# Attention with a feed-forward part in float32: four of eight key tiles in high and low parts, and rotations spread one per chunk

## The reference

```python
qkv = einsum('bsd,od->bso', xn, w_qkv)            # 16 heads of 128, q, k and v
q, k = rope(q), rope(k)                           # x*cos + rotate_half(x)*sin
attn = softmax(einsum('bqhd,bkhd->bhqk', q, k) / sqrt(128))
out = einsum('bhqk,bkhd->bqhd', attn, v)
att = einsum('bso,do->bsd', out.reshape(B, S, 2048), w_out)
h = gelu(xn @ dequantised(up) + up_bias)          # 256 -> 1024, weights rounded to MXFP4
ffn = h @ dequantised(down) + down_bias           # 1024 -> 256
```

## Time and profile before

| | us |
|---|---|
| median of 3 runs | 2452.34 (2449.78 to 2453.95) |
| the profiled execution's own time | 2450.13 |
| its span, first to last instruction | 2448.3 |
| PE busy | 2417.7 (99%) |
| DVE, POOL, ACT busy | 1912.9, 1728.9, 1677.9 |
| mean granted TensorE clock | 0.998 |

### The profile page before, as it was taken

The page is one execution under the profiler, slowest core; times in us unless marked ns, Lnnn a source line. Parts: engine busy times, 40 slices in busy tenths (PEclk is TensorE's granted clock), DMA queues, the critical chain, the costliest instruction groups (busy, mean ns, idle before and its releaser), DMA issues. The chain is left out here.

```text
span 2448.3 us, 42812 instructions
## 1 busy us (share of the span) xinstructions
PE 2417.7 (99%) x13168; PEld 2124.8 (87%) x13168; DVE 1912.9 (78%) x2671; ACT 1677.9 (69%) x3039; POOL 1728.9 (71%) x1358
## 2 busy tenths in 40 slices
PE   6999999999999999999999999999999999999999
PEld 5888888888888888888888888888888888888888
DVE  6778788777877877787787778778777877877776
ACT  7767777776766777676677767667776766777533
POOL 4778877777777777777777777777777777777331
PEclk9999999999999999999999999999999999999999
DMA  4766666667666666667666666667676565666742
GB/s 140 185 170 161 171 158 178 162 162 195 182 161 149 158 152 157 157 148 195 179 161 153 157 157 148 161 149 183 165 186 157 148 162 149 157 153 161 230 153 69
DMA packets 400878, 396.72 MB, mean 162 GB/s; under 512 B 38656, under 2 KB 383104, under 8 KB 400768
## 3 DMA queue, kind: packets, MB, share of 16 engines
q1 hardware_dynamic: 400768, 395.67, 63.0%
HBM read 91.43 MB, written 35.65 MB: 52 GB/s over the span
## 5 line engine op out<-in xcount | busy, mean ns | idle before, releaser
L947 DVE TENSOR_REDUCE neg_max<-s_ps 128x1 f32<-128x1024 f32 x512 | 621.0, 1219 | 291.2 <-PE s_ps L1244 290.5
L1244 PE MATMUL s_ps<-seq_parts 128*128 128x512 f32 x3072 | 826.8, 408 | 1.4 <-DVE seq_parts L1111 0.8
L758 ACT ACTIVATE probs<-s_ps,neg_max 128x1024 f32<-128x1024 f32 x512 | 570.6, 1114 | 365.5 <-DVE neg_max L947 361.8
L1326 PE MATMUL o_ps<-keys_first,v_rows 128*128 128x256 f32 x3072 | 707.7, 380 | 1.3 <-ACT v_rows L725 1.3
L957 DVE STREAM_TRANSPOSE turned_blocks<-probs 128x1024 f32<-128x1024 f32 x512 | 630.6, 1237 | 60.6 <-ACT probs L758 38.1
L1244 PEld LDWEIGHTS s_ps<-seq_parts 128*128 128x128 f32 x3072 | 571.8, 188 | 117.2 <-ACT probs L758 1.5
L1326 PEld LDWEIGHTS o_ps<-keys_first,v_rows 128*128 128x128 f32 x3072 | 566.9, 190 | 68.6 <-ACT v_rows L725 1.7
L608 POOL TENSOR_TENSOR keys_first<-keys_first,seq_parts 128x512 fp32r<-128x512 f32 x256 | 332.4, 1298 | 320.2 <-ACT seq_parts L764 320.0
L587 POOL TENSOR_TENSOR rope_a<-rope_a,cos 128x512 f32<-128x512 f32 x252 | 325.3, 1291 | 176.9 <-ACT rope_b L740 176.7
L601 POOL TENSOR_TENSOR seq_parts<-rope_a,seq_parts 128x512 fp32r<-128x512 f32 x252 | 359.4, 1426 | 95.2 <-ACT seq_parts L750 95.1
L1244 PE MATMUL slot_ps<-seq_parts,w_parts 128*128 128x512 f32 x1506 | 387.9, 393 | 0.0
(11 more groups left out here) (118 smaller groups left out, 2597.2 us busy)
## 6 DMA issues: line engine op xcount, KB each, us to landing
keys_first<-turned_blocks SPq DMA_DIRECT2D x2048, 128.0 KB, 2.7
w_parts<-w_qkv_parts SPq DMA_DIRECT2D x72, 512.0 KB, 4.3
w_qkv_parts<-w_parts SPq DMA_DIRECT2D x24, 512.0 KB, 3.7
wo_parts<-w_out_parts SPq DMA_DIRECT2D x48, 256.0 KB, 3.1
seq_parts<-xnt_parts SPq DMA_DIRECT2D x16, 512.0 KB, 4.6
w_raw<-in_w_qkv SPq DMA_DIRECT2D x24, 256.0 KB, 4.1
seq_parts<-xnt_parts SPq DMA_DIRECT2D x6, 1024.0 KB, 8.5
y<-in_x SPq DMA_DIRECT2D x16, 256.0 KB, 3.2
```

Source lines behind the costliest of these rows:

```text
L758: nc.scalar.activation(probs[:, k2 % 4, :], s_ps[k2 % 2][:, :], ACT.Exp, bias=neg_max[:, col:col + 1], accum_out=row_sum[:, col:col + 1]). ...
L947: nc.vector.tensor_reduce(neg_max[:, k2 % 16:k2 % 16 + 1], s_ps[k2 % 2][:, :], AXX, ALU.max, negate=True).then_inc(max_ready, 1)
L1244: ins = nc.tensor.matmul(out, w, m, start=(n == 0), stop=(n == len(terms) - 1))
L1326: last = nc.tensor.matmul(out, v_rows[:, parity, kt - SPLIT, cols], keys_first[:, slot, :, kt, :].bitcast(F32), start=False, stop=(kt == B ...
```

## The change

It has four parts.

1. `SPLIT` goes from 2 to 4: four of eight key tiles are done in parts in all chunks. `values` has 12 fp32r matmuls and 4 plain ones instead of 6 and 6; `probs_high` rounds 1024 columns in one instruction instead of 512; `probs_low` becomes two instructions of 512 columns with a semaphore each, and PE waits for both before its first matmul on a low part. A second projection of values per pair (`v` 0) needs a `v_low`.
2. Rotations: in each step POOL does `probs_low`, one `rotated_low` and one `rotated_sum`, and ACT does one `rotated_high` behind `probs_high`. For this the projections move: `qk0` 0 goes from step 2 to step 1, and so on by about a step; `v` 3 goes from (1, 0) to (0, 0), so step 1 still has one projection, now in slot 1. The take of `qk1` 0 (step 5) stands behind the second exponential.
3. In the first sequence the parts of the `qk1` weights are made in step 3 instead of 4; the loads of the next sequence's `xnt` are issued a step earlier.
4. The end: the high parts of the probabilities now fill the memory of the feed-forward part's `g_hi`, so of the first group only two `up` stand in the last chunks, and everything else of it behind them.

```diff
-SPLIT = 2
+FRONT_TILES, SPLIT = 2, 4
...
-        GROUPS = {(2, 1): (0, "qk0", 0), (3, 1): (1, "qk0", 1), (4, 0): (2, "qk0", 2), (4, 1): (3, "v", 0),
...
+        GROUPS = {(1, 1): (0, "qk0", 0), (2, 1): (1, "qk0", 1), (3, 1): (2, "qk0", 2), (4, 0): (3, "v", 0),
...
+        FIRST_LATER = {(0, 0): (9, "qk1", 2), (0, 1): (10, "qk1", 3), (1, 0): (11, "v", 3)}
+        SUM_AT = {2: ("qk0", 0), 3: ("qk0", 1), 4: ("qk0", 2), 5: ("qk0", 3), 6: ("qk1", 0), 7: ("qk1", 1), 0: ("qk1", 2), 1: ("qk1", 3)}
+        LOW_AT = {(k + 1) % 8: g for k, g in SUM_AT.items()}
...
+        FRONT, BACK = slice(0, FRONT_TILES), slice(FRONT_TILES, SPLIT)
+        USED = {"qk0": 5, "v": 12, "qk1": 12}
...
-            ahead = k // 8 + (1 if k % 8 >= 2 else 0)
+            ahead = k // 8 + (1 if k % 8 >= 1 else 0)
...
-                    for at, part in ((0, "qk0"), (2, "v"), (4, "qk1")):
+                    for at, part in ((0, "qk0"), (2, "v"), (3, "qk1")):
...
-                low = keys_first[:, slot, :, 0:SPLIT, :]
-                nc.gpsimd.tensor_tensor(low, low.bitcast(F32), p_hi[:, slot, :, :, :].bitcast(F32),
-                                        ALU.subtract).then_inc(p_lo_ready, 1)
+                low = keys_first[:, slot, :, FRONT, :]
+                nc.gpsimd.tensor_tensor(low, low.bitcast(F32), p_hi[:, slot, :, FRONT, :].bitcast(F32),
+                                        ALU.subtract).then_inc(p_lo_front, 1)
+                low = keys_first[:, slot, :, BACK, :]
+                nc.gpsimd.tensor_tensor(low, low.bitcast(F32), p_hi[:, slot, :, BACK, :].bitcast(F32),
+                                        ALU.subtract).then_inc(p_lo_back, 1)
...
-                if k8 == 0:
+                if first and k == 0:
                     rotated_low(p, "qk1", 0)
                     rotated_sum(p, "qk1", 1)
                     rotated_sum(p, "qk1", 2)
-                if k8 == 1:
+                elif first and k == 1:
                     rotated_low(p, "qk1", 1)
                     rotated_low(p, "qk1", 2)
                     rotated_sum(p, "qk1", 3)
-                if k8 == 2:
-                    rotated_low(p, "qk1", 3)
-                if k8 == 3 and more_pairs:
-                    rotated_sum(p + 1, "qk0", 0)
-                if k8 == 4 and more_pairs:
-                    rotated_low(p + 1, "qk0", 0)
-                    rotated_sum(p + 1, "qk0", 1)
-                if k8 == 5 and more_pairs:
-                    rotated_low(p + 1, "qk0", 1)
-                    rotated_sum(p + 1, "qk0", 2)
-                if k8 == 6 and more_pairs:
-                    rotated_low(p + 1, "qk0", 2)
-                    rotated_sum(p + 1, "qk0", 3)
-                    rotated_low(p + 1, "qk0", 3)
-                if k8 == 7 and more_pairs:
-                    rotated_sum(p + 1, "qk1", 0)
+                else:
+                    if k8 < 3 or more_pairs:
+                        rotated_low(p if k8 < 3 else p + 1, *LOW_AT[k8])
+                    if k8 < 2 or more_pairs:
+                        rotated_sum(p if k8 < 2 else p + 1, *SUM_AT[k8])
                 if k == 2:
                     guess(i + 2, LN_COLS)
                 if k8 == 0 and more:
                     w_low(p + 1, "qk0")
                 if k8 == 2 and more:
                     w_low(p + 1, "v")
+                if k8 == 3 and more:
+                    w_low(p + 1, "qk1")
                 if k8 == 3 and splitting:
                     wo_low(p, 1)
-                if k8 == 4 and more:
...
-                if tail:
-                    if k == 16:
-                        gelu(0, 2, True)
-                        gelu(0, 3, True)
-                    else:
-                        high_out(c - 2, k % 2)
-                    return
...
-                if g_before and k % 8 != 1:
+                g_before = None if tail or (first and k == 0) else group_at(k - 1, 1, last, first)
+                if g_before and not (first and k == 1):
...
-                    if k % 8 == 2:
-                        rotated_high(p, "qk1", 3)
-                    g = group_at(k, 0, last)
-                    if g:
+                    g = group_at(k, 0, last, first)
+                    if g and k % 8 != 5:
                         take(0, g)
-                    if k % 8 == 1:
+                    if first and k == 1:
                         rotated_high(p, "qk1", 2)
-                    if k % 8 == 1 and g_before:
                         take(1, g_before)
-                    if k % 8 == 6 and more_pairs:
-                        rotated_high(p + 1, "qk0", 3)
                     if not (last and k == 15):
                         exponentials(t + 3, 2 * k + 3, first and k == 0)
-                    if k % 8 == 3 and more_pairs:
-                        rotated_high(p + 1, "qk0", 0)
-                    if k % 8 == 4 and more_pairs:
-                        rotated_high(p + 1, "qk0", 1)
-                    if k % 8 == 5 and more_pairs:
-                        rotated_high(p + 1, "qk0", 2)
-                    if k % 8 == 7 and more_pairs:
-                        rotated_high(p + 1, "qk1", 0)
-                    if k % 8 == 0:
+                    if g and k % 8 == 5:
+                        take(0, g)
+                    probs_high(i, k)
+                    if first and k == 0:
                         rotated_high(p, "qk1", 1)
-                    if last and k == 15:
-                        act.wait_ge(bias_loaded, 32)
-                        act.wait_ge(blocks_turned, TOK * HEADS // P - 3)
-                        gelu(0, 0, True)
-                        gelu(0, 1, True)
-                        high_out(c - 1, 0)
-                    probs_high(i, k)
+                    elif k % 8 < 2 or more_pairs:
...
+                        rotated_high(p if k % 8 < 2 else p + 1, *SUM_AT[k % 8])
...
-            for f in range(4, FT):
+            act.wait_ge(bias_loaded, 32)
+            act.wait_ge(blocks_turned, TOK * HEADS // P)
+            for f in range(FT):
...
-                if k == 16 and tail:
-                    split_gelu(0, 0, True)
-                    split_gelu(0, 1, True)
...
-                if k == 17 and tail:
-                    dve.wait_ge(o_ready, BATCH * SEQ_CHUNKS)
-                    split_gelu(0, 2, True)
-                    split_gelu(0, 3, True)
...
-                pe.wait_ge(p_lo_ready, c + 1)
+                pe.wait_ge(p_lo_front, c + 1)
+                pe.wait_ge(p_lo_back, c + 1)
...
-                if last and k == 15:
-                    up(0, 0, 0)
-                    up(0, 0, 1)
-                elif tail and k == 16:
-                    up(0, 0, 2)
-                    pe.wait_ge(mx_w_loaded[1], 32)
-                    pe.wait_ge(probs_ready, TOK * HEADS // P)
-                    down(0, 0, 0)
-                elif tail:
-                    down(0, 0, 1)
+                if tail:
+                    up(0, 0, k - 16)
...
-            pe.wait_ge(mx_w_loaded[2], 16)
+            pe.wait_ge(mx_w_loaded[1], 48)
+            pe.wait_ge(probs_ready, TOK * HEADS // P)
...
```

54 lines of the change are left out of this document (25 added, 29 removed).

## The result

The changed kernel took 2496.2 us (median of 4 runs, 2488.8 to 2498.0), the kernel before 2451.65 beside it: ratio 1.0176, 95% interval 1.0153 to 1.0198. The forecast was 2441 us, with a range of 2420 to 2463.

A forecast was written before the change was run, and what follows sets the result against it. PE's own work was taken to set the time. Terms: -35.8 + 10.8 + 2.4 + 9.1 - 2 + 4.8 = -10.7 us from 2450.13 profiled, 2441 us given; the forecast's own range 2432 to 2449, overall 2420 to 2463.

The forecast's parts named there:

- Gain on PE: Two key tiles per chunk go from plain to fp32r matmuls: 0.14 us less per chunk, 35.8 us over 256 chunks.
- POOL in the sum: The second `probs_low` adds 10.4 us of POOL work per pair; the total fits, 89% later, 97% in the first sequence.
- DVE behind POOL: DVE's small SBUF instructions run long while POOL works, delaying `low_out`: 0.1 us per pair, 2.4 us; bounds nothing and 22.
- my own model of step 3: Later sequences: PE loses 0.45 us waiting for slot 1's bank; the first turn ends earlier, leaving about 0.5 us at `low_out`.
- the ACT paragraph: Its `low_out` sum: the subtraction ends at 2.6 us in the step, output matmuls begin at 2.94, so not late.
- DVE is late everywhere: Rival: `low_out` 0.9 us late in two of three one-projection steps, 1.8 us lost per pair; 2479 us, chance 0.16.
- ACT and the bank of slot 1: Step 3: ACT's longer work empties the bank late, PE loses 0.45 us per pair in 24 pairs, 10.8 us.
- First sequence: ACT also rounds weights: 1.3 us lost per pair in 7 pairs, 9.1 us; some 2 us of existing gaps go.
- The end: Behind the last chunks, two `up` and two `down` remain and PE stands about 1.1 us: 4.8 us lost; bounds 3 and 8.

The follow-up runs named there:

- the run with fewer instructions: The changed kernel with the four `v_lo` products of each chunk left out and one full-precision product put in: 2469.3 us, ratio 1.0068.
- the spread refinement: The changed kernel with the refinement in three operations, two a step earlier, and the first pair's early projection one step later: 2475.1 us, ratio 1.0098.

## Why the prediction was wrong

- **Gain on PE: right.** A step with one projection takes 8.03 us, 0.13 less; undisturbed pairs take 70.3, where 70.15 was worked out.
- **POOL in the sum: right in size, wrong in what it was asked.** I asked whether `p_lo` comes in time for PE. It does: no wait of 0.4 us or more in the pairs is put down to it. What the fuller POOL does to DVE I looked at in one place only.
- **DVE behind POOL: the step that failed.** It stood at 2.4 us with bounds 0 and 22; `o_lo` waits came to 37.5 us (15.8 + 9.3 + 6.9 + 5.5). I took the price per place (0.9 us; measured, on average, 0.8 and 0.9 in steps 11 and 4, but 1.4 in step 5 and 2.3 in step 3) from one place, and the number of places from my own model of step 3. No row backs the 0.5 us that this model leaves at `low_out`; the ACT paragraph has 2.6 against 2.94, 0.34. The trace of before had the list: the DVE instructions on SBUF whose minimum lies far under 1.3 us, above all chains of them in a row. The refinement (four in a row, the last of them 161 ns in the median before) never came up, because before it cost nothing. Taking three of the four out gave 23 us back.
- **The rival "DVE is late everywhere"** (2479 us) had the mechanism, not the places: it put the loss into steps of each pair, the trace has it once a round and in the first sequence.
- **Not in the prediction at all: PE's instructions.** Two records more a chunk (six fp32r matmuls more, two plain ones of two records each less) pushed the loop body from 774 to 806, over the room; 14.4 us (with the cheaper products taken off, the run with fewer instructions gives 27 - 12 = 15).
- **Not in the prediction: the start,** 5.5 us, though the diff gave step 1 a projection in a bank that ACT empties late there. One moved table entry undid it (-6.5 us).
- **ACT and the bank of slot 1:** 0.45 us in each of 24 pairs forecast, 10.8; it came as 0.42 in 10 of the second pairs of rounds (step 11, 4.2 us) and 2.4 in step 4. The size of one wait was right; that half of them fell to other waits, which had already delayed PE, is my reading and was not tested.
- **First sequence:** +9.1 - 2 forecast; step 3 waits some 2.4 us, not 1.0, but in four pairs only (9.3). The forecast put it on ACT's weights and the bank; it was `o_lo`; the timelines show it behind MX operations under POOL (1.37 and 1.26 us above). No run took these out, so this is read and not tested.
- **The clock** was in no term: up to 6.8 us, each time behind a long wait.
- **The end: right,** 4.2 against 4.8 us.

Still open: the 8 us or more of delays too small to trace singly, and why some kernels with 806 matmuls reload in 6 to 9 of 14 repeats and others in all. Not run: two pieces and the spread refinement together with a body that fits; from 2475.1 - 27 it would lie near 2448 (an estimate), level with the kernel before, with 12 of the 27 us from products left out.

## What to carry to other kernels

Before filling an idle GpSimd, list VectorE's short instructions on SBUF and give each one running GpSimd instruction as its length (the reduction above was an exception); what counted here is chains of them ahead of something TensorE needs, and how long a single GpSimd instruction is, not only its share. Count the instructions of an unrolled TensorE loop body before adding to it, and look at the instruction queue's packets: here a body just over the room cost a pause in 6 to 14 of 14 rounds. Cost the first round of a pipeline by itself.
